# GNN layers on one core: one wait on POOL's own completion for four scatters in place of one for two

## The reference

```python
def _L0(x, edge_index, W1, b1, W2, b2):
    row, col = edge_index                       # src, dst
    feat = concat([x[col], x[row] - x[col]], -1)
    m = relu(feat @ W1 + b1) @ W2 + b2
    out = segment_max(m, col, num_segments=N)   # -inf -> 0
    return out
def _L1(x, edge_index, W1, b1, W2, b2, Wres, bres):
    src, dst = edge_index
    h = x + segment_sum(x[src], dst, num_segments=N)
    return (x @ Wres + bres) + relu(h @ W1 + b1) @ W2 + b2
x = layernorm(x + _L0(x, ...)); x = layernorm(x + _L1(x, ...)); return x
```

## Time and profile before

| | us |
|---|---|
| median of 3 runs | 1343.35 (1338.25 to 1344.81) |
| the profiled execution | 1332.02 |
| its span | 1330.2 |
| POOL busy | 825.8 (62%), 797 instructions |
| TensorE (PE) busy | 1123.7 (84%) |
| VectorE (DVE) busy | 1068.6 (80%) |

### The profile page before, as it was taken

The page is one execution under the profiler, slowest core; times in us unless marked ns, Lnnn a source line. Parts: engine busy times, 40 slices in busy tenths (PEclk is TensorE's granted clock), DMA queues, the critical chain, the costliest instruction groups (busy, mean ns, idle before and its releaser), DMA issues. The chain is left out here.

```text
span 1330.2 us, 32137 instructions
## 1 busy us (share of the span) xinstructions
PE 1123.7 (84%) x7512; PEld 853.2 (64%) x7512; DVE 1068.6 (80%) x5491; ACT 799.8 (60%) x2305; POOL 825.8 (62%) x797
## 2 busy tenths in 40 slices
PE   2699999998888878788759999999999999999500
PEld 1577777765555545455448888888887777777400
DVE  6599999989887887898838999999987888888400
ACT  0366666666665656667526666666666777777400
POOL 5666666656666666666256666666665666655654
PEclk9899999999998999999979999999999999999855
DMA  4477777756665667666436565656564556656310
GB/s 111 141 220 214 214 220 212 222 188 195 183 208 180 199 174 210 177 205 196 141 112 191 187 185 186 185 187 187 189 190 140 177 181 190 185 181 200 103 38 28
DMA packets 160366, 233.86 MB, mean 176 GB/s; under 512 B 26815, under 2 KB 69273, under 8 KB 160284
## 3 DMA queue, kind: packets, MB, share of 16 engines
q1 hardware_dynamic: 133612, 193.69, 46.7%
q0 software_dynamic: 25088, 38.81, 11.0%
q10 hardware_dynamic: 1584, 0.53, 0.2%
HBM read 129.48 MB, written 90.12 MB: 165 GB/s over the span
## 5 line engine op out<-in xcount | busy, mean ns | idle before, releaser
L1277 PE MATMUL psY<-wcr,xT 128*128 128x128 f32 x1568 | 305.0, 276 | 0.0
L1276 PE MATMUL psY<-wc,hT 128*128 128x128 f32 x1568 | 304.6, 276 | 0.0
L586 POOL DMA_INDIRECT edge_rows<-x1e_table,idx x196 | 210.8, 1075 | 133.2 <-DMA edge_rows<-x1e_table,idx 77.6
L593 POOL DMA_INDIRECT out<-edge_rows,idx x196 | 202.2, 1031 | 129.5 <-issue 76.4
L586 POOL DMA_INDIRECT edge_rows<-in_x,idx x196 | 206.9, 1056 | 116.0 <-DMA edge_rows<-in_x,idx 67.3
L586 POOL DMA_INDIRECT xd_rows<-in_x,idx x196 | 203.5, 1038 | 115.9 <-DMA xd_rows<-in_x,idx 67.3
L1276 PEld LDWEIGHTS psY<-wc,hT 128*128 128x128 f32 x1568 | 255.8, 193 | 15.0 <-issue 8.3
L1123 ACT ACTIVATE o_rows<-psY,rs_b 128x128 f32<-128x128 f32 x784 | 223.0, 367 | 66.7 <-DVE rs_b L741 66.5
L1277 PEld LDWEIGHTS psY<-wcr,xT 128*128 128x128 f32 x1568 | 239.9, 193 | 0.0
L1287 PE MATMUL psH<-xT,wc 128*128 128x512 f32 x392 | 204.5, 604 | 16.0 <-DVE deltas L787 10.6
L1103 ACT ACTIVATE sd_a<-mv_a,eps_col 128x4 f32<-128x4 f32 x196 | 58.3, 298 | 239.6 <-DVE mv_a L677 239.6
(11 more groups left out here) (135 smaller groups left out, 2042.6 us busy)
## 6 DMA issues: line engine op xcount, KB each, us to landing
x_in<-in_x SPq DMA_DIRECT2D x196, 256.0 KB
out<-o_rows SPq DMA_DIRECT2D x196, 256.0 KB
xs_rows<-edge_rows SPq DMA_DIRECT2D x98, 256.0 KB, 2.9
xs_rows<-src_dram SPq DMA_DIRECT2D x49, 256.0 KB, 4.3
mask<-mask_dram SPq DMA_DIRECT2D x98, 128.0 KB, 3.6
x1e_table<-shared SPq DMA_DIRECT2D x49, 256.0 KB, 2.8
x1eT_spill<-x1eT SPq DMA_DIRECT2D x49, 256.0 KB
x1eT<-x1eT_spill SPq DMA_DIRECT2D x49, 256.0 KB, 2.8
```

Of the source, the lines that this page charges most:

```text
L586: nc.gpsimd.indirect_dma_start(to, None, table, bass.IndirectOffsetOnAxis(idx[:, what, t:t + 1], 0), bounds_check=rows - 1, oob_is_err=err ...
L593: nc.gpsimd.indirect_dma_start(table, bass.IndirectOffsetOnAxis(idx[:, SCAT, t:t + 1], 0), frm, None, bounds_check=N - 1, oob_is_err=False ...
L1276: t_.matmul(to[:, cut(t)], h[:, cut(t)], wc2[:, :], start=False, stop=False, skip_group_check=True)
L1277: last = t_.matmul(to[:, cut(t)], xt[:, cut(t)], wcr[:, :], start=False, stop=t == TILES - 1, skip_group_check=True)
```

## The change

The pacing gets a burst length. Gathers keep two, scatters have four: only the fourth scatter of a group carries `engine_sem`, and only behind it does POOL wait. `pauses` counts the waits, since the semaphore is now raised 294 times by the gathers and 49 times by the scatters. All other waits of a group stay where they were.

```diff
-            def pace(kw):
+            pauses = [0]
+            GATHERS_A_BURST, SCATTERS_A_BURST = 2, 4
+
+            def pace(kw, burst):
                 issued[0] += 1
-                if issued[0] % 2 == 0:
+                if issued[0] % burst == 0:
                     kw["engine_sem"] = s_issued
-
-            def issued_pair():
-                if issued[0] % 2 == 0:
-                    pool.wait_ge(s_issued, issued[0] // 2)
+                    pauses[0] += 1
+
+            def issued_burst(burst):
+                if issued[0] % burst == 0:
+                    pool.wait_ge(s_issued, pauses[0])
...
             def scatter(table, frm, t, done):
                 kw = {}
-                pace(kw)
+                pace(kw, SCATTERS_A_BURST)
                 nc.gpsimd.indirect_dma_start(table, ..., **kw).then_inc(done, 16)
-                issued_pair()
+                issued_burst(SCATTERS_A_BURST)
```

More of the change, by code:

```diff
@@ L570, in _ @@
             issued = [0]
-            def pace(kw):
+            pauses = [0]
+            GATHERS_A_BURST, SCATTERS_A_BURST = 2, 4
+            def pace(kw, burst):
                 issued[0] += 1
-                if issued[0] % 2 == 0:
+                if issued[0] % burst == 0:
                     kw["engine_sem"] = s_issued
-            def issued_pair():
-                if issued[0] % 2 == 0:
-                    pool.wait_ge(s_issued, issued[0] // 2)
+                    pauses[0] += 1
+            def issued_burst(burst):
+                if issued[0] % burst == 0:
+                    pool.wait_ge(s_issued, pauses[0])
             def gather(to, table, what, t, done):
                 kw = {}
-                pace(kw)
+                pace(kw, GATHERS_A_BURST)
                 rows, err = (GROUPS * ROWS, False) if what == PLACE else (N, True)
@@ L587, in gather @@
                                              bounds_check=rows - 1, oob_is_err=err, **kw).then_inc(done, 16)
-                issued_pair()
+                issued_burst(GATHERS_A_BURST)
             def scatter(table, frm, t, done):
                 kw = {}
-                pace(kw)
+                pace(kw, SCATTERS_A_BURST)
                 nc.gpsimd.indirect_dma_start(table, bass.IndirectOffsetOnAxis(idx[:, SCAT, t:t + 1], 0), frm, None,
                                              bounds_check=N - 1, oob_is_err=False, **kw).then_inc(done, 16)
-                issued_pair()
+                issued_burst(SCATTERS_A_BURST)
             def gather_src(g):
```

## The result

| | before | after |
|---|---|---|
| median | 1340.8 us (4 runs, 1337.31 to 1344.81) | 1393.72 us (4 runs, 1390.77 to 1398.16) |
| ratio | | 1.0396, 95% interval 1.0349 to 1.0444 |
| span of the profiled execution | 1330.2 | 1388.9 |

What follows compares the result with a forecast made beforehand. POOL's serial scatters were taken to bound the kernel. Removing 49 waits (25.0 us) and fewer collisions with VectorE (5 us) were to save 30 us: 1343.35 to 1313 us, range 1303 to 1334.

Steps and rivals of the forecast that it cites:

- What bounds the kernel: POOL's scatters to the end: 329.6 us of its own serial work, each microsecond saved there being one off the time.
- 49 waits at 0.51 us: Ahead of each group's third scatter: the gap falls from 0.81 to 0.30 us, saving 25.0 us.
- Fewer collisions with VectorE's scale: Scatters beside the dense work: fewer are held by VectorE's scale, a further gain taken as 5 us.
- Who else could be late: Other waits of the scatter groups, dense stores included: none becomes late; the last group keeps 23 us of room.
- the sum: Whole kernel: 25.0 + 5 = 30 us off the median of 1343.35, giving 1313 us.
- The rivals: For POOL's scatters: in step with dense units again, 1331 (0.10); third keeps old gap, 1343 (0.11); burst stalls, 1380 (0.09).
- the slower one: POOL's third or fourth scatter stalls for lack of descriptor room, gap like 1.56 us: 37 us lost, 1380 us; chance 0.09.

Runs made afterwards that it cites:

- e5: Scatters in bursts of three instead of the pairs of the kernel before, gathers still in pairs: 1313.01 us, ratio 0.9833.
- late window: Kernel before with pairs up to group 39, then at most one scatter queued behind the running one: 1323.36 us (ratio 0.9919) and, on another chip, 1333.79 us (0.9955).
- e3: Against the kernel before, each scatter waits for the last but one, so one is always queued, in all groups: 1479.5 us, ratio 1.1005.
- e2: The changed kernel with every scatter index out of range, so no rows are moved: 1385.54 us (one run).
- e12: The changed kernel without any value_load, store counts being constants rounded up: 1512.96 us, ratio 1.1068 to the kernel before.
- e15: Against the kernel before, scatters in threes up to group 39, then at most one queued behind the running one: 1430.84 us, ratio 1.0441.
- e19: The changed kernel, unaltered, run once more on another chip: 1458.24 us, ratio 1.0677 to the kernel before.

## Why the prediction was wrong, step by step

*What bounds the kernel*: right. POOL's serial scatters set the end of the kernel before.

*49 waits at 0.51 us*: right in size. The gap is 0.30 to 0.31 ahead of the second, third and fourth. It is this that shows that a third and fourth are taken early; the memsets of the earlier trace rows, which overlap, did not. The run that shows what a wait is worth is e5: 33 waits fewer, 16.8 us by the same price, and POOL's idle time ahead of scatters fell by 17.7 (129.5 to 111.8).

*Fewer collisions with VectorE's scale*: right in mechanism and size. The scatters' busy time came down from 202.2 to 196.7 in after and 196.8 in e5; about 197 was forecast. In after a slower dense path helped to that; e5 is the clean case, with threes. Its scatters took 23.0 us less than the 329.6 of before. The medians say 22.2 less (1335.23 - 1313.01), the two profiled executions 17.4, since the one of e5 was 5.7 us later at its first scatter, so that the match of 16.8 + 5.4 with 22.2 is in part luck.

*Who else could be late*: this step failed. It took the dense stores' schedule from before, with the last at 1252.9, found 23 us of room and put the cost to the dense work at nothing. It asked what a faster POOL needs from the dense work, and not what POOL's pauses had given to it. The last store came at 1371.8, and POOL then waited for it. The schedule was no constant: on the same chip it ends at 1294.3 with pairs, 1339.8 with threes, 1378.3 with fours. What the sum left out is therefore the late signals of TensorE: 92.1 us of dense work behind the 120th store, against which stand the 30 us that POOL was to gain. With it falls the sentence that each microsecond saved in POOL's scatters is one off the time: that held in e5, not here.

*The rivals*: the slower one put the stall on POOL's own third scatter. POOL never stalled there. A rival on TensorE's signals was missing, and nothing in the profile of before hinted at its price, since that profile is from a chip of the kind where signals aren't late. One row could have warned: the profiled execution took 1332.0 where all three runs shown took 1338 to 1345. I wrote that no row explains it and carried on.

## What to carry to other kernels

A wait on an engine's own completion can be of use to other engines: before taking it out of a stretch, compare their signals (end of the producer against start of an idle consumer), not the waiting engine's timeline alone, and first take it out only where nobody else works, as the late window did (0.5 to 0.8%; on the second kind it still began some 20 us before the last dense store of pairs). When a profiled time lies outside the range of the timed runs, find out on what the runs were made before the rows are trusted for them. Threes would have been called a gain of 1.7% from one chip and a loss of 2.0% from another; a change to pacing needs runs on both.

## What was not expected of the hardware

While POOL worked through indirect DMAs without a pause, waits of up to 17.6 us on TensorE's signals stood on VectorE (e3); with fours they came with no rows moved just as well as with them (e2). Only TensorE's signals were late: ScalarE's updates stand 0.01 us behind their instructions in every trace, and of VectorE's three are over 1 us late (1.4 to 1.7, one each in e3, e12 and e15). A `value_load` in the pause between bursts lengthened the pause from 1.08 to 1.63 us, and the loss was 2.3% instead of the 6.8 of e19, on chips where before takes about the same.
